# Expert logits by row-times-column on VectorE, and one program block for cross-attention and expert products, in a decoder layer

## The reference, cut to what matters

```python
x = x + self_attention(layernorm(x), w_qkv, w_out)
# cross-attention, for n = layernorm(x)
q = n @ wq.T
k, v = concat(ctx, n @ wk.T), concat(ctx, n @ wv.T)
x = x + softmax(q @ k.T / sqrt(512)) @ v @ wo.T
# experts
xt = layernorm(x).reshape(2048, 512)
logits = xt @ wg                      # 2048 x 8
probs = softmax(logits); idx = argmax(probs); gate = probs[idx]
x = x + gate * (xt @ W[idx].T + b[idx])
```

## Time and profile before

| what | value |
|---|---|
| median of 3 runs | 758.77 us (758.11 to 762.05) |
| the profiled execution's own time | 760.28 us |
| its span, first to last instruction | 758.4 us |
| mean granted clock of TensorE | 0.958 of full speed |
| self-attention | 0 to 342.7 us |
| cross-attention, batches 0 to 6 | 342.8 to 612.5 us |
| cross-attention, last batch | 612.5 to 654 us |
| products of the experts | 665.7 to 758.4 us |

### The profile page before, as it was taken

One profiled execution on the slowest core, in us unless ns is written; L12 is line 12 of the kernel. 1 busy time (PEld: TensorE's weight loads), 2 busy tenths in 40 slices (PEclk: granted clock), 3 DMA queues, 4 the chain that ended last, 5 costly groups with the idle time before them and its releaser, 6 DMA issues. The chain is left out here.

```text
span 758.4 us, 19014 instructions
## 1 busy us (share of the span) xinstructions
PE 682.1 (90%) x6040; PEld 606.2 (80%) x6041; DVE 501.7 (66%) x1478; ACT 309.4 (41%) x985; POOL 330.4 (44%) x558
## 2 busy tenths in 40 slices
PE   4768999999999999999999999999999986379995
PEld 4757898989888878878899999999999965257884
DVE  4767788888787878846555555556564559464663
ACT  3445565666655666623132323232323263012220
POOL 4376757575766786714101010101010155654652
PEclk9879999999999999999999999999999998579998
DMA  6477875655656657719914233343420245366530
GB/s 249 147 153 136 118 145 116 149 133 126 141 123 135 139 112 137 180 43 309 328 38 113 54 113 53 111 55 111 55 105 6 73 121 193 85 103 217 177 103 13
DMA packets 142744, 95.09 MB, mean 125 GB/s; under 512 B 110702, under 2 KB 114926, under 8 KB 142576
## 3 DMA queue, kind: packets, MB, share of 16 engines
q1 hardware_dynamic: 137040, 82.00, 45.3%
q0 software_dynamic: 5664, 12.61, 6.1%
HBM read 56.14 MB, written 18.77 MB: 99 GB/s over the span
## 5 line engine op out<-in xcount | busy, mean ns | idle before, releaser
L508 ACT ACTIVATE prob<-prob,shift 128x128 f32<-128x128 f32 (+1 forms) x256 | 114.5, 449 | 116.6 <-POOL shift L419 116.1
L1302 ACT CAST w_hi<-b_bank 128x256 fp32r<-128x256 f32 (+1 forms) x132 | 56.4, 445 | 161.0 <-PE b_bank L60 139.6
L60 PE MATMUL b_bank<-w_hi 128*128 128x256 f32 (+1 forms) x536 | 110.5, 329 | 5.7 <-DVE w_lo L1472 5.7
L60 PE MATMUL a_job<-w_hi 128*128 128x256 f32 (+1 forms) x488 | 94.5, 317 | 16.0 <-DVE w_lo L711 7.6
L60 PE MATMUL b_bank<-w_lo,w_hi 128*128 128x256 f32 (+1 forms) x536 | 107.0, 322 | 0.0
L60 PE MATMUL b_bank<-w_hi,w_lo 128*128 128x256 f32 (+1 forms) x536 | 106.2, 320 | 0.0
L732 DVE CUSTOM_DVE_ANT_0 prob<-a_s,mask 128x128 f32<-128x128 f32 (+1 forms) x256 | 79.6, 347 | 30.1 <-PE a_s L608 29.9
L1472 DVE TENSOR_TENSOR w_lo<-b_bank,w_hi 128x256 fp32r<-128x256 f32 (+1 forms) x132 | 63.0, 507 | 50.8 <-ACT w_hi L1302 50.3
L60 PEld LDWEIGHTS b_bank<-w_hi 128*128 128x128 f32 x536 | 82.9, 193 | 12.6 <-DVE w_lo L1472 3.7
L60 PEld LDWEIGHTS a_job<-w_hi 128*128 128x128 f32 x488 | 71.3, 195 | 25.8 <-DVE w_lo L711 8.2
L60 PEld LDWEIGHTS b_bank<-w_lo,w_hi 128*128 128x128 f32 x536 | 84.1, 192 | 7.9
(11 more groups left out here) (173 smaller groups left out, 1149.7 us busy)
## 6 DMA issues: line engine op xcount, KB each, us to landing
stage<-in_w SPq DMA_DIRECT2D x6, 1024.0 KB, 8.4
xin<-in_x SPq DMA_DIRECT2D x8, 512.0 KB, 4.2
xr<-in_x SPq DMA_DIRECT2D x8, 512.0 KB, 3.9
x<-xr SPq DMA_DIRECT2D x8, 512.0 KB, 3.2
xin<-x SPq DMA_DIRECT2D x8, 512.0 KB, 9.6
xr<-x SPq DMA_DIRECT2D x8, 512.0 KB, 4.4
x2n<-x_sb SPq DMA_DIRECT2D x8, 512.0 KB
x2n<-xn_sb SPq DMA_DIRECT2D x8, 512.0 KB, 6.9
```

Of the source, the lines that this page charges most:

```text
L60: ins = pe_matmul(out, a, b, start=first and i == 0, stop=last and i == len(steps) - 1)
L508: a = nc.scalar.activation(prob[:, e % NPROB, cols], prob[:, e % NPROB, cols], ACT.Exp, scale=-1.0, bias=shift[:, e, q:q + 1], accum_out=r ...
L1302: nc.scalar.copy(hi, src).then_inc(job_hi, 1)
```

## The change

There are three parts to it.

**The logits.** In batches 0 to 6 the jobs `Y0 Y1 l0 l1` are gone from the list, which leaves 22 jobs. DVE makes each logit column itself. A "dot" (`dot`) multiplies the 512 channels of 128 tokens by one column of `wg`, which lies in every partition (`wg_all`, 2 MB, loaded into `bias_sb`), and sums over the channels. There are 16 dots in a batch, 8 experts times 2 tiles. Table `DOTS` says behind which jobs they stand: seven behind k1 to v1 of their own batch, nine between X1 and q2 of the next. In batch 6 all 16 stand behind k1 to v1 (`LAST_DOTS`). The last batch keeps Y and l on TensorE.

**One block.** The products are a class whose parts are appended to each engine's program in the cross-attention block. They use four of the 7 banks, and xin and xn for their results.

**The last batch and the weights.** The last batch has a hand-written order on DVE (`last_batch`), with its norm and routing tile by tile; `choose` is split into `choose` and `gates`. The context of the cross-attention lies in stage 2. The experts' weights use the buffers in another order, and experts 2, 3, 7 and 6 are loaded when the last dot is done.

```diff
+CONTEXTS = 2
...
+    def gates(self, nc, dve, n):
+
+        done = n * self.STEPS
...
-    BUFFER = (0, 1, 2, 3, 4, 0, 1, 2)
+    BUFFER = (0, 1, 4, 3, 2, 0, 2, 1)
+
+    HIGH_ORDER = (0, 1, 2, 4, 3, 5, 7, 6)
...
-        cin = sb("cin", [P, TB, D])
-        cin_t = sb("cin_t", [P, DC, S])
+
+        wg_all = bias_sb[:].rearrange("p (e n) -> p e n", e=E)
+        unwanted = sb("unwanted", [P, 2, D], BF16)
+        wg_all_in, dots_done = sem("wg_all_in"), sem("dots_done")
+
+        flat = stage[CONTEXTS][:].rearrange("p c n -> p (c n)")
+        cin = flat[:, 0:TB * D].rearrange("p (t n) -> p t n", t=TB)
+        cin_t = flat[:, TB * D:].rearrange("p (c n) -> p c n", c=DC)
...
-        ORDER = ("X0 X1 s0 s1 q0 q1 p0 p1 q2 q3 o0 o1 o2 o3 k0 y0 y1 k1 k2 k3 v0 Y0 Y1 v1 l0 l1").split()
+        ORDER = ("X0 X1 s0 s1 q0 q1 p0 p1 q2 q3 o0 o1 o2 o3 k0 y0 y1 k1 k2 k3 v0 v1").split()
         FRONT = "Xqkv"
...
+        DOTS = {"k1": 1, "k2": 1, "k3": 1, "v0": 2, "v1": 2, "+X1": 1, "+s0": 1, "+s1": 2, "+q0": 1, "+q1": 1, "+p0": 1,
+                "+p1": 1, "+q2": 1}
+        LAST_DOTS = {"k1": 2, "k2": 2, "k3": 2, "v0": 5, "v1": 5}
+        assert sum(DOTS.values()) == sum(LAST_DOTS.values()) == TB * E
+
+        def dots_behind(j, n):
+
+
+            whole = LAST_DOTS if isinstance(n, int) and n == B - 2 else DOTS
+            def part(dots, key):
+                first = sum(c for i, c in enumerate(dots.values()) if i < list(dots).index(key)) if key in dots else 0
+                return range(first, first + dots.get(key, 0))
+            return part(whole, j), part(DOTS, "+" + j) if has_routing(n) else ()
+
+        LAST = "s0 s1 p0 p1 o0 o1 o2 o3 y0 y1 Y0 l0 Y1 l1".split()
...
-            for e in (0, 1, 2, 4):
+            for e in (0, 1):
                 experts.load(sp, w, e)
             sp.wait_ge(wo_split, 2)
-            experts.load(sp, w, 3)
+            sp.dma_start(bias_sb[:], bass.AP(tensor=wg_t.tensor, offset=wg_t.offset, ap=[[0, P], [1, E * D]]))\
+                .then_inc(wg_all_in, 16)
...
             batch(0, True, True)
             with sp.Fori(1, B - 2) as n:
                 batch(n, True, True)
+            sp.wait_ge(ct_split, B - 1)
+            sp.wait_ge(c_split, B - 1)
+            experts.load(sp, w, 4)
             batch(B - 2, True, False)
-            batch(B - 1, False, False)
+            experts.load(sp, w, 5)
+            sp.wait_ge(dots_done, (B - 1) * TB * E)
+            for e in (2, 3, 7, 6):
+                experts.load(sp, w, e)
             sp.wait_ge(blocks.known_done, 2)
             sp.wait_ge(routing.entries_in, 16 * TB * (B - 1))
             for k in range(Blocks.KNOWN):
                 blocks.entries(sp, routing.table, 0, k)
+            for e in (2, 3):
+                experts.wait_split(sp, e)
+            sp.dma_start(bias_sb[:], bass.AP(tensor=bias.tensor, offset=bias.offset, ap=[[0, P], [1, E * D]]))\
+                .then_inc(bias_in, 16)
+            batch(B - 1, False, False)
+            products.sync(sp)
...
+            experts.low(nc.gpsimd, 0)
             rstd_ln3(B - 2)
             routing.store_entries(nc, pool, tick_pool, B - 3)
             experts.low(nc.gpsimd, 1)
             routing.next_tokens(nc, pool, tick_pool, B - 3)
-            for e in (2, 4):
+            experts.low(nc.gpsimd, 2)
+            routing.store_entries(nc, pool, tick_pool, B - 2)
+            for e in (4, 3):
                 experts.low(nc.gpsimd, e)
-            routing.store_entries(nc, pool, tick_pool, B - 2)
-            experts.low(nc.gpsimd, 5, (0, 1))
-            rstd_ln3(B - 1)
-            experts.low(nc.gpsimd, 5, (2, 3))
-            experts.low(nc.gpsimd, 6)
             routing.next_tokens(nc, pool, tick_pool, B - 2)
             for stored in x2n_out:
                 pool.wait_ge(stored, 16 * (B - 1))
-            for k in (0, 1):
-                blocks.first_gather(nc, pool, tick_pool, experts, k)
+
+            def rstd_tile(t):
+                pool.wait_ge(ln3_dve, (B - 1) * 5 + 3 * (t + 1))
+                nc.gpsimd.tensor_tensor(rstd[:, 1, t:t + 1], veps[:, 1, t:t + 1], expo[:, t:t + 1], ALU.pow)\
+                    .then_inc(ln3_rstd, 1)
+
+            blocks.first_gather(nc, pool, tick_pool, experts, 0)
+            rstd_tile(0)
+            blocks.first_gather(nc, pool, tick_pool, experts, 1)
+            rstd_tile(1)
+            products.pool(pool)
+
+
+        FREE = {("q3", B - 2): (0,), ("k3", B - 2): (1,), ("v1", B - 2): (2,), ("p1", B - 1): (4, 3), ("o3", B - 1): (5, 7)}
...
+            batch(B - 2)
+            routing.exponentials(nc, act, B - 2)
             batch(B - 1)
...
+            def dot(i, n):
+
+                e, t = divmod(i, TB)
+                if i == 0:
+                    dve.wait_ge(xn3_ready, (n + 1) * TB)
+                    dve.sem_inc(tick, 1)
+
+                if i >= 2 or has_routing(n):
+                    dve.wait_ge(dots_done, n * TB * E + i - 1)
+                    dve.sem_inc(tick, 1)
+                nc.vector.tensor_tensor_reduce(out=unwanted[:, i % 2, :], in0=xn3_sb[:, t, :], in1=wg_all[:, e, :], scale=1.0,
+                                               scalar=0.0, op0=ALU.mult, op1=ALU.add,
+                                               accum_out=routing.logits[:, t, e:e + 1]).then_inc(dots_done, 1)
...
+                    if j == "k1":
+                        wait(dve, xn3_out, 16 * n)
+                        dve.wait_ge(ln3_rstd, n + 1)
+                        norm_apply(1, xn3_sb, x2_sb, xn3_ready)
+                    own, before = dots_behind(j, n)
+                    for i in own:
+                        dot(i, n)
+                    for i in before:
+                        dot(i, n - 1)
...
+            def last_batch(n):
+
+                dve.wait_ge(dots_done, n * TB * E)
+                dve.sem_inc(tick, 1)
+                routing.choose(nc, dve, n - 1)
+                scores_max("s0", n)
+                scores_max("s1", n)
+                routing.gates(nc, dve, n - 1)
+                lo_part("p0", n)
+                lo_part("p1", n)
+                routing.place_tokens(nc, dve, n - 1)
+                nc.vector.reciprocal(rinv[:], rsum[:]).then_inc(rinv_done, 1)
+                blocks.known_blocks(nc, dve, routing)
+                for j in ("o0", "o1", "o2", "o3"):
+                    lo_part(j, n)
+                experts.low(nc.vector, 5)
+                add_output("y0", n)
+                tile_stats(0, n)
+                experts.low(nc.vector, 7, (0, 1))
+                tile_apply(0, n)
+                add_output("y1", n)
+                tile_stats(1, n)
+                move_rows("Y0", n)
+                tile_apply(1, n)
+                experts.low(nc.vector, 7, (2,))
+                move_logits("l0", n)
+                move_rows("Y1", n)
+                experts.low(nc.vector, 7, (3,))
+                experts.low(nc.vector, 6, (0,))
+                move_logits("l1", n)
+                dve.wait_ge(job_ev, ev_at("l1", n))
+                dve.sem_inc(tick, 1)
+                routing.choose(nc, dve, n)
+                experts.low(nc.vector, 6, (1, 2, 3))
+                routing.gates(nc, dve, n)
+                routing.place_tokens(nc, dve, n)
+
+            dve.wait_ge(wg_all_in, 16)
...
             batch(0)
             dve.wait_ge(routing.consts, Routing.CONSTS)
             with dve.Fori(1, B - 2) as n:
                 batch(n)
             batch(B - 2)
-            experts.low(nc.vector, 0)
-            batch(B - 1)
-
-
-def mixture_of_experts(nc, ident, routing, blocks, x2n_out, bias_sb, bias_in, out, experts):
-
-
-
+            last_batch(B - 1)
+            products.dve(dve)
...
+class Products:
...
+        for k in range(2, AHEAD):
+            blocks.first_gather(nc, pool, tick_pool, experts, k)
+        routing.store_entries(nc, pool, tick_pool, B - 1)
...
+            if k == self.FIRST:
+                for stored in x2n_out:
+                    pool.wait_ge(stored, 16 * B)
...
+        def step(i, k):
+            transposes(i, k)
+            if isinstance(i, int) and k == 0:
+                routing.count(nc, pe, B - 1)
+            if isinstance(i, int) and k == 1:
+                experts.all_split(pe)
+            if k >= 1:
+                product(i, k - 1)
```

More of the change, by code:

```diff
@@ L1173, in route_after @@
         def route_after(n):
[L1174 removed]
+            return "q3"
         def bank(j, n):
@@ L1521, in batch @@
                         ctx_lo(n + 1)
-                    if order(n) is LAST and j in LOWS:
-                        experts.low(nc.vector, *LOWS[j])
-                    if order(n) is LAST and j == "o3":
-                        blocks.known_blocks(nc, dve, routing)
                     if j == "p1":
@@ L1749, in program @@
-def program(nc, x, ctx, ctx_t, w_qkv, w_out, wq, wk, wv, wo, wg, w, bias, out):
+        self.nc, self.ident, self.routing, self.blocks, self.experts = nc, ident, routing, blocks, experts
```

(30 more changed lines are left out.)

447 lines of the change are left out of this document (217 added, 230 removed).

## The result

The changed kernel takes **787.76 us** (median of 4 runs, 786.13 to 791.44) against 759.6 us of the kernel before on the same chip (758.11 to 762.05): a ratio of **1.0373**, 95% interval 1.0338 to 1.0408. The profiled execution has a span of 785.7 us, 27.3 more than the 758.4 of before. Predicted were 777 us and a span 17.6 longer.

The account below looks back on a forecast made before the run. TensorE, busy 90% of the span, was taken as the bound, with a serial chain from the last batch and DVE's lateness. Terms 22 - 2.8 + 2 + 5.4 - 9 = +17.6 us on 758.4 gave 777 us, range 766 to 790.

Parts of the forecast that it names:

- term E: From s0 of the last batch to the end: expert 2's load +4.3, boundary -9.5, serial rest -5; sum -9 us.
- term D: Batch 6 finishes its own 16 dots, some slowed beside POOL's splits of experts 0 and 1: +5.4 us (2 to 9).
- the prediction's own case: The predicted mechanism holds: 768 to 787 us, chance 0.62.
- rival (2): TensorE's clock falls at the new pauses: about 788 us, with both pauses 798; chance 0.15.
- Term A: Opening of cross-attention: DVE waits for the wg load, +19 us, then TensorE's slow clock, +3; together +22.
- B: Batch 0, without dots of an earlier batch: -2.5 + 1.5, and a pause of 1.76 goes; -2.8 us.
- What every batch saves: TensorE drops the Y transposes (0.79) and logits (1.70): 2.5 us a batch; DVE gains 16 dots of 0.65.
- Rival (3): DVE becomes the bound of whole batches if a dot costs 0.84 us or more: 785 to 795 us, chance 0.08.
- The two new waits: TensorE waits before X0 for v1's bank, +1.5 us, and at o0 behind three dots, +1.4 us.
- Term C: Batches 1 to 5: -2.5 + 1.5 + 1.4 = +0.4 us each, +2 in all (up to +8).
- The second reading that the prediction gave: In batch 6 an exclusive port lock makes a dot wait for a whole POOL piece each time: term D's upper end.
- Rivals (4) and (5): (4): larger gains, no slow start, 766 us, chance 0.11; (5): opening load early, DVE's wait covered, about 754, chance 0.04.

Follow-up runs that it names:

- the first experiment: Changed kernel with DVE's wait for the load of wg moved from the program's head to the first dot: ratio 1.0078 to the kernel before.
- the other bank: Changed kernel with job v1 in PSUM bank 4 in place of bank 0: ratio 1.0263 to the kernel before.
- the moved dots: Changed kernel with the dots behind q0 and q1 moved to behind v0 and s0: ratio 1.0283 to the kernel before.
- the gaps: Changed kernel with POOL waiting for its own instruction after each piece of a split of expert weights: ratio 1.0307 to the kernel before.
- the second profile: Changed kernel run again unchanged: ratio 1.0348 to the kernel before, span 789.4 us.
- the last kernel: Kernel with all five edits, but batch 6's logits on PE, experts 2 and 3 loaded earlier, expert 2's high part behind v1: 0.9709 to the kernel before.
- the kernel with all edits: Changed kernel with wg wait at first dot, v1 in bank 4, dots moved, POOL's pieces apart, expert 2's high part behind p1: 0.9771, again 0.9811, to kernel before.

## Why the prediction was right, and where it fell short

The sign, the largest term and the two waits of every batch were right, in size and in mechanism. The sum was 9.7 us short (17.6 against 27.3): 6.8 of it lie in term E and 2.6 in term D, and in both a mechanism was wrong. The measured 787.8 us lie just above the 768 to 787 of the prediction's own case and on the 788 of rival (2), so the number alone could not have told the two apart; the clock in the trace does.

- **Term A, the opening (+22) with B (-2.8): right.** 18.7 together against 19.2. The choice between 6.6 us of traffic and 12.5 to landing was measured as 8.1. DVE starts at 367.45 (predicted 366.7), `q0` at 368.80 (368.1), after a pause of 19.00. The clock was 0.50 behind it. X0 to `q0` grew by 19.2 (19 predicted), which leaves 2.3 for the slow clock (3). That nearly the whole of it hangs on where the wait stands is shown by the first experiment.
- **What every batch saves (-2.5) and the dots: right.** A dot has 0.61 us from start to start (0.65 taken, 0.84 the bound). DVE is busy 30.76 us in a batch, 31.5 predicted. Rival (3) is out.
- **The two new waits: right.** 1.48 before X0 (1.5) and 1.17 before o0 (1.4), shown one by one by the other bank and the moved dots. Term C is +2.3 against +2.
- **Rival (2), the clock, is out.** Pauses of 1.48 and 1.17 recur in every middle batch, and the clock is 1.00 there.
- **Term D (+5.4): +8.0.** The step that failed is the one on five dots "so slowed" beside POOL by the ratio of 1.18 to 0.69, which with the small operations was priced at 3.3. One dot waited for the whole run of POOL's four pieces, 4.9 us more than its own length, and the others ran at full speed. The second reading that the prediction gave, an exclusive lock, gives the better size, since it puts the term at its upper end. But back to back the dots did not wait for a piece each, as that reading had it; they did so in the first experiment and with the gaps (1.1 to 1.9 us a dot). By difference another 1 us is left, so DVE's spare time was less than the 2.2 counted. And terms D and E are not apart here: with v1 in another bank s0 came earlier and p0 did not.
- **Term E (-9): -2.2, and about +2.5 in the second profile, by its longer products.** By its steps the wait for expert 2's load was +3.6 (+4.3), the norm tile by tile -4.5 (-5) and the boundary -9.3 (-9.5). The step that failed is "known_blocks (DVE) covers part", +1 for the stretch from p0 to y0: it measured +7.2. known_blocks was thought to be cover; one of its operations took 10.35 us beside POOL's splits of experts 4 and 3, ahead of low parts that `y0` needs. With one block and PE logits, the gaps moved y0's pause from 8.88 to 4.41 and the time from 1.0003 to 0.9929.
- **Rivals (4) and (5)** had nothing in the traces for them: the gains were smaller, and the opening wait was as long as said.
- **Two small slips of arithmetic** change nothing: 776.0 and 0.4 make 776.4 and not 777, and the chances of (1) to (4) less 0.02 make 0.94 and not 0.93.

The Trainium skill, "SBUF — State Buffer", section "SBUF: two separate sides", has whichever of the two starts first hold the shared pair "for the whole instruction; the other fully blocks". The traces agree that it is a lock, and mostly one of a single instruction: 1.15 us beside expert 0's split, 1.77 in the first experiment. In two places they go further: a DVE operation waited for four pieces (5.53 us) and another for eight (10.35 us) that followed each other without a wait.

**What stays open.** What decides between the two cases isn't known. The waits for more than one piece are of three kinds in the profiles, and all began within 0.5 us of the start of POOL's run: the dot 0.02 us behind it, and the operation of 7 columns 0.45 us ahead of it, while POOL was still storing entries. The third is in the kernel before, 3.11 us beside two pieces, begun 0.48 ahead of them and also during a store. All that began further into a run waited for one piece at most. But the dot that began 0.05 us ahead of the run in the first experiment was not held up, so the start alone doesn't decide it. The gaps between POOL's pieces moved y0 by 4.9 us behind p0, but of the time it is only known that they gave about 3 to 5 us, with intervals that overlap. What makes the products vary between 92.8 and 98.7 us wasn't found; so how much of the earlier y0 is given back in them can't be told. Nor was it tried how far the last kernel's remaining pause of 5.46 before y0 can be closed.

## What to carry to other kernels

Moving work from a full engine to one with idle time pays only where its place in the other engine's queue is right, whatever the sum of busy times says: put a wait for a load at the first use and not at the head of the program, look at the banks again when a list of jobs gets shorter, and put the new work behind the operations that others wait for. When POOL streams through SBUF back to back, look at every DVE operation on SBUF beside it, however small and with one tensor input too, and at what is queued behind it. When an edit removes a pause, look whether the next one grows by as much, as p0's did with the other bank. Where the receiving engine is crowded or a buffer is held too long by the move (here batch 6), leave that part of the work where it was.

## What the runs showed of the hardware

- Beside back-to-back operations of POOL, DVE operations mostly waited for one of them: 1.15 us for a TENSOR_TENSOR of 16 columns, 1.77 for a dot of the first experiment, whose POOL run took 6.81 us for 4.99. A dot that began 0.02 us behind the first of four waited for all four, 5.53 us.
- A DVE operation of 7 columns took 10.35 us beside eight back-to-back operations of POOL, 1.92 us when POOL waited for itself between them, and 0.17 us in the kernel with all edits, where POOL had none under way. A TENSOR_SCALAR of 7 columns with one tensor input went from 0.17 us to 1.25 beside the spaced ones.
- The multiply-and-reduce instruction at 512 columns, float32 in and bfloat16 out, takes 0.68 us, 0.61 from start to start; the read of its accumulator (0.08) is hidden.
- A load of 2 MB that gives one row to all partitions landed 8.1 us behind its issue at the opening, where the same form had taken 12.5 us for the bias.
- After 19.00 us without work TensorE ran at 0.50 of its clock for the 5 us of the window shown; recurring pauses of 1.48 and 1.17 us left it at 1.00.
